# The self parts of a graph layer added to its residual in DRAM

## The reference, cut to what matters

```python
h = maximum(layernorm(x), 0)
x1 = x + (h @ W.T + bias)                 # W scattered from the edge weights
h = maximum(layernorm(x1), 0)
# two layers; A is the 1250 x 1250 matrix of edge counts, dinv = 1 / max(degree, 1)
h1  = relu(h  @ W_self0 + dinv * (A @ (h  @ W_neigh0)) + b0)
out =      h1 @ W_self1 + dinv * (A @ (h1 @ W_neigh1)) + b1
return x1 + out
```

## Time and profile before

| | |
|---|---|
| time, median of 3 runs | 789.57 us (789.22 to 791.21) |
| the profiled execution | 792.57 us, its span 790.7 us |
| TensorE matmul busy | 749.0 us, 95% of the span |
| VectorE busy | 576.4 us, 73% |
| GpSimd busy | 474.7 us, 60% |
| ScalarE busy | 354.8 us, 45% |
| mean granted TensorE clock | 0.987 of full |
| DMA | 148.82 MB, 188 GB/s over the span |

### The profile page before, as it was taken

How to read it: one execution, slowest core, us unless ns; L and a number is a source line. 1 busy time by engine, 2 the same in 40 slices (tenths; PEclk the granted TensorE clock), 3 DMA queues, 4 the chain that set the end, 5 groups by cost and what they waited for, 6 DMA issues and landing times.

```text
span 790.7 us, 13483 instructions
## 1 busy us (share of the span) xinstructions
PE 749.0 (95%) x4433; PEld 618.9 (78%) x4434; DVE 576.4 (73%) x813; ACT 354.8 (45%) x596; POOL 474.7 (60%) x593
## 2 busy tenths in 40 slices
PE   2878999999999999999998999999999999999998
PEld 2767888888878787788886888888878888877876
DVE  7989377778555799976676775446588867689595
ACT  7756743343244267632335655443222223245631
POOL 5000057666758899674765382417799765754884
PEclk9689999999999999999999999999999999999999
DMA  3112455865675862565865625966853668775277
GB/s 113 43 52 93 132 166 193 257 197 184 196 233 192 285 199 94 167 208 193 294 211 170 187 93 151 279 217 197 288 160 110 201 222 279 253 240 191 102 214 274
DMA packets 82877, 148.82 MB, mean 188 GB/s; under 512 B 10795, under 2 KB 20898, under 8 KB 82800
## 3 DMA queue, kind: packets, MB, share of 16 engines
q1 hardware_dynamic: 62862, 105.07, 42.4%
q10 hardware_dynamic: 19938, 42.79, 15.2%
HBM read 106.42 MB, written 41.41 MB: 187 GB/s over the span
## 4 chain that ended last, share of the span: by engine, by line
PE 69%; POOL 10%; DVE 10%; issue 7%; DMA 2%; ACT 1%; SPq 0%; POOLq 0%; DVEq 0%; ACTq 0%
PE bank L1713 33%; PE bank L1760 20%; PE bank L1647 12%; POOL split L1097 3%; DVE L L1943 3%; POOL T L1114 3%; DVE R L1928 2%; POOL T L1112 2%; DMA stage<-hT_scratch 2%; DVE L L1935 1%; POOL S L1083 1%; PE bank L1543 1%; PE bank L1559 1%; PE bank L1776 1%; PE bank L1640 1%
## 5 line engine op out<-in xcount | busy, mean ns | idle before, releaser
L1713 PE MATMUL bank<-slot,split 128*128 128x512 f32 x1680 | 386.7, 390 | 2.5 <-POOL split L1097 1.7
L1713 PEld LDWEIGHTS bank<-slot,split 128*128 128x128 f32 x1680 | 313.6, 188 | 69.4 <-issue 4.6
L1059 POOL TENSOR_TENSOR AT<-AT,az 128x50 int32 (+3 forms) x288 | 96.5, 335 | 121.6 <-DMA az<-asum_scratch 79.3
L1760 PE MATMUL bank<-slot,Ax 128*128 128x512 f32 x500 | 119.1, 392 | 2.4 <-DVE slot L2184 1.4
L1097 POOL TENSOR_TENSOR split<-stage,split 128x512 fp32r<-128x512 f32 x50 | 66.9, 1340 | 77.9 <-ACT split L1322 76.1
L1760 PEld LDWEIGHTS bank<-slot,Ax 128*128 128x128 f32 x500 | 92.9, 188 | 22.2 <-DVE slot L2184 1.8
L2080 DVE TENSOR_TENSOR slot<-T,slot 128x512 fp32r<-128x512 f32 x64 | 90.9, 1448 | 9.7 <-ACT slot L1313 8.3
L1647 PE MATMUL bank<-slot,split_m 128*128 128x512 f32 x320 | 91.1, 396 | 0.0
L1322 ACT CAST split<-stage 128x512 fp32r<-128x512 f32 x50 | 31.1, 623 | 121.9 <-PE bank L1713 74.2
L1114 POOL TENSOR_TENSOR T<-T,wst 128x512 f32<-128x512 f32 x48 | 68.7, 1447 | 4.6 <-DMA wst<-in_L_gnn_W_self 4.6
L1647 PEld LDWEIGHTS bank<-slot,split_m 128*128 128x128 f32 x320 | 58.5, 188 | 11.0
(11 more groups left out here) (219 smaller groups left out, 1124.7 us busy)
## 6 DMA issues: line engine op xcount, KB each, us to landing
stage<-hT_scratch SPq DMA_DIRECT2D x90, 256.0 KB, 3.5
wst<-in_L_gnn_W_neigh SPq DMA_DIRECT2D x56, 256.0 KB, 4.5
wst<-in_L_gnn_W_self SPq DMA_DIRECT2D x56, 256.0 KB, 3.3
x1b_scratch<-x ACTq DMA_DIRECT2D x10, 512.0 KB, 5.5
hT_scratch<-hTs ACTq DMA_DIRECT2D x10, 512.0 KB, 3.4
wst<-prod0g_scratch SPq DMA_DIRECT2D x20, 256.0 KB, 3.5
hT_scratch<-h1s ACTq DMA_DIRECT2D x20, 256.0 KB, 3.3
wst<-prod1g_scratch SPq DMA_DIRECT2D x20, 256.0 KB, 3.4
```

The source lines that it names most:

```text
L1059: pool.tensor_tensor(a, a, az32[:, n % NZ, pairs * pos:pairs * (pos + 1)], ALU.add) \
L1713: last = pe.matmul(dense_bank(v, which)[:, :], split[:, v % 2, a, NT * k:NT * (k + 1)], slot[t % 2][:, b, HF * (HK * which + k):HF * (HK * ...
L1760: last = pe.matmul(sums, Ax[:, u % NR_A, NT * k:NT * (k + 1)], part, start=(begins and k == 0 and b == 0), stop=(k == PAIRS - 1 and b == 1 ...
```

## The change

In the second layer the self parts are no longer stored to a scratch tensor of their own. GpSimd's queue issues a transfer for each that adds it to the x1 tile in DRAM (`dma_start` with `accum_op=ALU.add` into `x1b_scratch`), 20 of them with 256 KB each. `add_to_x1(v - 1)` stands at the end of GpSimd's iteration v, behind `right_lo`; the one for the last product stands behind the low parts of T2. It waits for VectorE to have taken product v - 1, and for the adding transfer two before it (`s_added` has two semaphores, used in turn). The A stage's `load_sums` loads one tile for each output, and `add_x1` and VectorE's L2264 are gone in it. Those who waited for a self store to free its source, namely VectorE in `sub_products`, `first_sums` and `take`, and ScalarE in `keep_first_A`, wait for the adding transfer. The stores of the neighbour parts and the first layer's stores stay on ScalarE's queue. In the first layer, a difference that counted a semaphore `s_a3` is counted as a link in VectorE's own chain, and ScalarE waits for the sum made from it in its place.

```diff
...
@@ -561,9 +560,20 @@
 
             return 16 * (PAIRS // 2 + 1 - i % 2) * (2 * layer + (p == 5)) + 16 * (i // 2 + 1)
 
-        def wait_c22(eng, layer, which, tiles):
+        def nth_added(half, n):
+
+            i = n % PAIRS
+            if half == n // PAIRS:
+                return PAIRS + 2 * i if half else i
+            return 3 * PAIRS + i if half else PAIRS + 2 * i + 1
+
+        def wait_added(eng, half, n):
+            m = nth_added(half, n)
+            eng.wait_ge(s_added[m % 2], 16 * (m // 2 + 1))
+
+        def wait_c22(eng, layer, tiles):
             for i in tiles:
-                eng.wait_ge(s_cst[2 * (i % 2) + which], cst_stored(layer, 5, i))
+                eng.wait_ge(s_cst[2 * (i % 2)], cst_stored(layer, 5, i))
 
         def dense_bank(v, which):
             return bank[2 * (v % VL % 3) + which]
...
@@ -867,22 +878,17 @@
                 elif o == 0:
                     sp.wait_ge(s_olo, VL * (layer + 1))
                     wait_low(sp, layer, "B11", PAIRS - 1)
-                if o == 0 and layer == 1:
-                    for r in range(2):
-                        sp.wait_ge(s_h1d[r], used(OL - 2 + r, 2))
-                    for i in range(TN - 2, TN):
-                        sp.wait_ge(s_x1d[i % 2], used(i, 2))
-                if half == 0 and n >= PAIRS:
-                    sp.wait_ge(s_c21, 16 * PAIRS * (layer + 1))
+                if layer == 1:
+                    wait_added(sp, half, n)
+                elif half == 0 and n >= PAIRS:
+                    sp.wait_ge(s_c21, 16 * PAIRS)
                 elif half == 1 and n < PAIRS:
-                    sp.wait_ge(s_c12[n % 2], c12_stored(layer, n))
+                    sp.wait_ge(s_c12[n % 2], c12_stored(n))
                 elif half == 1:
-                    wait_c22(sp, layer, 1, [n - PAIRS])
+                    sp.wait_ge(s_cst[2 * (n - PAIRS) % 4 + 1], cst_stored(0, 5, n - PAIRS))
                 else:
-                    sp.wait_ge(s_cst[2 * (n % 2) + 1], cst_stored(layer, 1, n))
-                sp.dma_start(sums_tile(layer, o), prod_d[layer][1][half, n]).then_inc(s_sl[o % NO], 16)
-                if layer == 1:
-                    sp.dma_start(x1_tile(o), x1b_d[n][:, HF * half:HF * (half + 1)]).then_inc(s_sl[o % NO], 16)
+                    sp.wait_ge(s_cst[2 * (n % 2) + 1], cst_stored(0, 1, n))
+                sp.dma_start(sums_tile(layer, o), self_part(layer, half, n)).then_inc(s_sl[o % NO], 16)
 
             def load_bias(layer):
 
@@ -1124,10 +1130,19 @@
                 high, low_part = right(layer, what, k)
                 pool.tensor_tensor(low_part, unsplit(what, k), high.bitcast(F32), ALU.subtract).then_inc(s_low_g, 1)
 
-            def add_x1(o):
-
-                pool.wait_ge(s_sl[o % NO], sums_loaded(1, o))
-                pool.tensor_tensor(sums_tile(1, o), sums_tile(1, o), x1_tile(o), ALU.add).then_inc(s_xadd, 1)
+            def add_to_x1(v):
+
+                layer, p, i = parts(v)
+                if layer == 0 or p not in (1, 5, 6):
+                    return
+                pool.wait_ge(s_evd, nth_sub(v) + 1)
+                from_cst, from_q = cst[:, 2 * (i % 2) + 1, :], q[:, p // 6, 1, i, :]
+                for half, n, source in {1: [(0, i, from_cst)], 5: [(1, i + PAIRS, from_cst), (0, i + PAIRS, from_q)],
+                                        6: [(1, i, from_q)]}[p]:
+                    m = nth_added(half, n)
+                    if m >= 2:
+                        pool.wait_ge(s_added[m % 2], 16 * (m // 2))
+                    pool.dma_start(self_part(1, half, n), source, accum_op=ALU.add).then_inc(s_added[m % 2], 16)
 
             def first_block_lo(b):
 
@@ -1155,8 +1170,11 @@
                         right_lo(layer, "B11", r - VL + 2 * PAIRS - 1)
                     if r >= VL - 2:
                         right_lo(layer, "T1", r - VL + 2)
+                    if v > VL * layer:
+                        add_to_x1(v - 1)
                 for k in range(PAIRS):
                     right_lo(layer, "T2", k)
+                add_to_x1(VL * (layer + 1) - 1)
                 for k in range(2, PAIRS):
                     right_lo(layer, "T1", k)
                 for k in range(PAIRS):
@@ -1164,13 +1182,8 @@
                 for k in range(PAIRS):
                     right_lo(layer, "T3", k)
                 for k in range(PAIRS):
-                    if layer == 1 and k < PAIRS - 1:
-                        add_x1(PAIRS + k)
                     right_lo(layer, "T4", k)
-                if layer == 1:
-                    for o in range(2 * PAIRS - 1, OL):
-                        add_x1(o)
-                else:
+                if layer == 0:
                     for b in range(WB):
                         first_block_lo(b)
                     operand_lo(VL)
...
@@ -1394,7 +1407,10 @@
 
                 p, i = A_SEQ[u]
                 act.wait_ge(s_ag, VL * layer + u + 1)
-                act.wait_ge(s_c12[i % 2], c12_stored(layer, i))
+                if layer == 1:
+                    wait_added(act, 1, i)
+                else:
+                    act.wait_ge(s_c12[i % 2], c12_stored(i))
                 act.copy(first_A(i), a_bank_of(u)[:, :]).then_inc(s_first, 1)
 
             def keep_first(v):
@@ -1409,17 +1425,17 @@
                 if p not in (1, 5, 6):
                     return
                 act.wait_ge(s_evd, nth_sub(v) + 1)
-                for which in range(2):
-                    dest = prod_d[layer][which]
-                    if p == 1 or p == 5:
-                        act.dma_start(dest[p // 5, i + PAIRS * (p // 5)], cst[:, 2 * (i % 2) + which, :]) \
-                            .then_inc(s_cst[2 * (i % 2) + which], 16)
-                if p == 5:
-                    act.dma_start(prod_d[layer][1][0, i + PAIRS], q[:, 0, 1, i, :]).then_inc(s_c21, 16)
-                if p == 6:
+                if p < 6:
+                    half, n = p // 5, i + PAIRS * (p // 5)
+                    act.dma_start(prod_d[layer][half, n], cst[:, 2 * (i % 2), :]).then_inc(s_cst[2 * (i % 2)], 16)
+                    if layer == 0:
+                        act.dma_start(prod_s_d[half, n], cst[:, 2 * (i % 2) + 1, :]).then_inc(s_cst[2 * (i % 2) + 1], 16)
+                if p == 5 and layer == 0:
+                    act.dma_start(prod_s_d[0, i + PAIRS], q[:, 0, 1, i, :]).then_inc(s_c21, 16)
+                if p == 6 and layer == 0:
                     if i >= 2:
-                        act.wait_ge(s_c12[i % 2], c12_stored(layer, i - 2))
-                    act.dma_start(prod_d[layer][1][1, i], q[:, 1, 1, i, :]).then_inc(s_c12[i % 2], 16)
+                        act.wait_ge(s_c12[i % 2], c12_stored(i - 2))
+                    act.dma_start(prod_s_d[1, i], q[:, 1, 1, i, :]).then_inc(s_c12[i % 2], 16)
 
             def h1_out(o):
                 u, half, n = OUTS[o]
...
@@ -2191,7 +2210,10 @@
                 dve.tensor_tensor(t1, t1, staged("a", k), ALU.subtract).then_inc(s_sum_g, 1)
                 wait_staged(dve, layer, "b", k)
                 if k == 0:
-                    dve.wait_ge(s_c21, 16 * PAIRS * (layer + 1))
+                    if layer == 1:
+                        wait_added(dve, 0, TN - 1)
+                    else:
+                        dve.wait_ge(s_c21, 16 * PAIRS)
                 dve.wait_ge(s_sum_g, sum_made(layer, "T1", k))
                 dve.tensor_tensor(t2, staged("b", k), t1, ALU.subtract).then_inc(s_sum_g, 1)
 
...
@@ -2260,10 +2281,6 @@
                 half, n = OUTS[o][1:]
                 sums = sums_tile(layer, o)
                 dve.wait_ge(s_sl[o % NO], sums_loaded(layer, o))
-                if layer == 1 and o < PAIRS:
-                    link(dve.tensor_tensor(sums, sums, x1_tile(o), ALU.add))
-                elif layer == 1:
-                    dve.wait_ge(s_xadd, o - PAIRS + 1)
                 if p == 1:
                     return
                 if p == 5:
...
```

More of the change, by code:

```diff
@@ L155, in build_program @@
     asum_d = nc.dram_tensor("asum_scratch", (NS_A, P, AW * TN), U16, kind="Internal").ap()
-    prod_d = [[nc.dram_tensor(f"prod{layer}{which}_scratch", (2, TN, NT, HF), F32, kind="Internal").ap()
-               for which in "gs"] for layer in range(2)]
+    prod_d = [nc.dram_tensor(f"prod{layer}_scratch", (2, TN, NT, HF), F32, kind="Internal").ap() for layer in range(2)]
+    prod_s_d = nc.dram_tensor("prod_self_scratch", (2, TN, NT, HF), F32, kind="Internal").ap()
     hT_d = [nc.dram_tensor(f"hT{layer}_scratch", (TN, P, KT, NT), F32, kind="Internal").ap() for layer in range(2)]
@@ L423, in build_program @@
         s_as = sem("s_as")
-        s_a3 = sem("s_a3")
         s_turn = sem("s_turn")
@@ L429, in build_program @@
         s_evb = sem("s_evb")
-        s_xadd = sem("s_xadd")
         s_degs = sem("s_degs")
@@ L487, in build_program @@
         s_c21 = sem("s_c21")
+        s_added = [sem(f"s_added{i}") for i in range(2)]
         s_c12 = [sem(f"s_c12_{i}") for i in range(2)]
@@ L843, in load_b11 @@
```

(21 more changed lines are left out.)

11 lines of the change are left out of this document (6 added, 5 removed).

## The result

The changed kernel takes 801.86 us (median of 6 runs, 799.62 to 803.3), the kernel before beside it 790.91 us (6 runs, 789.22 to 791.88). The ratio is 1.0137, 95% interval 1.0114 to 1.016: 10.9 us slower. The prediction was 799.3 us, slower, with a sum of +9.7 us; by these times the loss is 1.2 us larger than that sum. The profiled execution of the changed kernel took 799.83 us, its span 797.9.

What follows compares the result with a forecast made beforehand. TensorE was taken as the bound, GpSimd next to it. 2.7 + 7.5 + 0.5 - 1.0 = +9.7 us (13g - 3.3) on the profiled 792.57 gives 802.3, 799.3 us on the runs' median scale; own range 793 to 802, widened to 789 to 811.

Steps and rivals of the forecast that it cites:

- The hold g: Time for which one GpSimd transfer issue holds up what stands behind it; taken as 1.0 us, halfway between 0.45 and 1.6.
- Rival 1: The issue hardly holds GpSimd, working beside its tensor instructions: 788.6 us, or 790.6 at g = 0.33; chance 0.23.
- rival 3: VectorE stretches GpSimd's issues 1.35 times: g = 1.35, sum +14.3 us, 803.9 us; chance 0.14.
- Step 1: Second layer: three issues fall where GpSimd works nearly without a break before 2.4's low part; 3g - 0.3 = 2.7 us.
- Step 5: Ten issues, two in each iteration 5.1 to 6.0, make GpSimd the bound for five products; 10g - 2.5 = 7.5 us.
- the waits for landing: Each issue waits for the adding transfer two before; landing taken as 5.3 us, fits step 5; VectorE's `first_sums` delayed, +0.5 us.
- rival 2: Landing bounds step 5: an adding transfer takes 9.1 us, 3 us more for four iterations, +12, 811 us; chance 0.13.
- The start of the A stage: VectorE, some 2.7 us late from waiting in 6.0 for the last of ten transfers, delays it: +0.5 us, bounds 0 and 4.
- The gain (a): A stage without the adds of x1: the TensorE gap of 0.99 us at 761.79 goes, -1.0 us, bounds 0 and -1.0.

Runs made afterwards that it cites:

- e9_hold: Kernel before, no transfer on GpSimd's queue, three memsets (1.05 us together) at each of the twenty places of the adding transfers: 798.38 us, ratio 1.0111.
- e3_no1: Changed kernel without the five adding transfers of step 1 (their self parts missing from the result): 797.65 us, ratio 1.0094 to the kernel before.
- e4_no5: Changed kernel without the ten adding transfers of step 5 (their self parts missing from the result): 793.63 us, ratio 1.0042 to the kernel before.
- e11_b11: e1_four with the five low parts of B11 in the second layer's step 5 moved from GpSimd to VectorE: 794.85 us, ratio 1.0067.
- e1_four: Changed kernel with four semaphores for the adding transfers, so an issue waits for the one four before it: 798.27 us, ratio 1.0095 to the kernel before.
- e12_third: As e9_hold, with one memset (0.31 us) at each place in place of three: 791.59 us, ratio 1.0029.
- e5_nox1: Kernel before without x1 in the second layer's A stage, neither loads nor adds: 789.31 us against 790.22, ratio 1.0000.
- e2_plain: Changed kernel with GpSimd's transfers as plain stores into their own tensor, the A stage loading and adding x1 as before: 800.56 us, ratio 1.0118.
- e10_read: As e9_hold, with three copies that read SBUF at each place in place of the memsets: 805.46 us, ratio 1.0213.
- e8_gap_four: e1_four with the issues ahead of the low part in GpSimd's iteration, not at its end: 807.43 us, ratio 1.0225.

## Why the prediction was right, and where its terms were off

**The mechanism is shown.** GpSimd is held at its queue in two stretches where it has no time to spare, and its low parts come late. In step 5 the hold alone is enough for it, in step 1 the transfers bring something more. A hold without any transfer makes 8.2 us (e9_hold, some 6.9 of it at the issue's own length), taking the issues out of a stretch takes out that stretch's gaps (e3_no1, e4_no5), and giving GpSimd time back does it too (e11_b11).

**The hold g**, taken as 1.0, is 0.88, between the bounds of 0.45 (as on ScalarE's queue) and 1.6 (as a tensor instruction). It is the same for both sources, median 864 and 865 ns, and beside a busy VectorE or not: 0.86 us at 570.10, beside a subtraction of VectorE, and 0.86 at 690.11, with VectorE idle. Rival 1 needed less than 0.44 and is out, and so is rival 3, VectorE stretching the issues. The rule of the Trainium skill named there ("SBUF — State Buffer", "Who interferes with whom") agrees with these rows.

**Step 1, forecast 3g - 0.3 = 2.7, measured 3.08.** The place is right, though the loss is spread over the gaps in front of 2.2, 2.3 and 2.4 and not in one. With the measured g my sum gives 2.3, and the trace has even less in the stretch that I counted: from the low part of 1.4 to that of 2.4 it is 589.88 - 558.95 = 30.93 us, 28.85 before, 2.08 more for three issues. The other 1.0 us was there before this stretch began, where I had written that the earlier issues are absorbed. The low part of 1.4 ended 48.42 us after the layer's first matmul before, and ends at 49.41. ScalarE's high part in front of it, in the kernel before and in the changed one, and GpSimd's low part:

```profile
558.76 0.62 ACT L1322 CAST split<-stage 128x512 fp32r<-128x512 f32 x1 [5.79 <-DMA stage<-hT_scratch]
```
```profile
556.89 0.62 ACT L1335 CAST split<-stage 128x512 fp32r<-128x512 f32 x1 [6.78 <-DMA stage<-hT_scratch]
557.66 1.29 POOL L1103 TENSOR_TENSOR split<-stage,split 128x512 fp32r<-128x512 f32 x1 [2.09 <-ACT split L1335]
```

GpSimd's idle time of 1.86 us was a wait for ScalarE, and ScalarE's for an operand load. That load came 0.98 us later, and SyncE began the row of loads with it 0.73 us later (at +41.23 against +40.50). e4_no5, with the same issues in step 1, has it 1.2 us late. In e3_no1, without them, it comes as before (+0.03). In e9_hold, with the hold and no transfer, it comes 2.0 us earlier than before, and step 1 loses only 1.1 us. So it isn't the hold that delays the load. That leaves the transfers themselves, their traffic or their waits; these are single traces, and no run separates the two.

Something else is new behind the hold. VectorE's row and GpSimd's in the changed kernel:

```profile
571.93 4.66 DVE L2187 TENSOR_TENSOR q<-q,b 128x512 f32<-128x512 f32 x1
```
```profile
574.46 1.57 POOL L1103 TENSOR_TENSOR split<-S,split 128x512 fp32r<-128x512 f32 x1
576.50 1.84 POOL L1085 TENSOR_TENSOR S<-stage 128x512 f32<-128x512 f32 x1 [0.47 <-DMA stage<-hT_scratch]
```

The same add took 0.87 us in the kernel before. It now ends at 576.59, 0.56 us after GpSimd's row of instructions, without a break since 564.67, breaks off at 576.03. A late GpSimd runs without breaks, and then can hold up VectorE. In the stretch above, this add cost TensorE nothing that the three issues don't cover.

**Step 5, forecast 10g - 2.5 = 7.5, measured 6.93, and here two errors met.** The hold itself costs less than I had it. e1_four, which has the hold without landing waits, shows it: from 2.4 to the A stage 120.19 us against 114.73 before, less 1.37 us of lower clock after its gap at 590.55, is 4.1. Three terms were too dear. The smaller g makes 1.2 us for ten issues. GpSimd's four iterations from the sum of 5.2 on took 683.63 - 661.84 = 21.8 us before; in e1_four they are 6.80, 6.81, 6.31 and 6.34, together 19.2 without 1.76 for each pair of issues. That is 2.6 us shorter, where my sum had 1.3, since GpSimd found ScalarE's second high part ready in the last two, as at 681.67 in the changed kernel, where it follows its low part without a wait. The third term was put at nothing: the wait for ScalarE's first high part of this kind, ahead of the first pair of issues, which shrank from 2.71 to 1.60 us (659.56 above), because ScalarE has no self parts to issue in front of it; in e9_hold, where it has them, the wait is 2.65. In the kernel before:

```profile
660.60 1.29 POOL L1125 TENSOR_TENSOR g_mid<-base,g_mid 128x512 fp32r<-128x512 f32 x1 [2.71 <-ACT g_mid L1391]
...
683.63 1.30 POOL L1088 TENSOR_TENSOR stage<-stage,S 128x512 f32<-128x512 f32 x1
```

7.5 less 1.2, 1.3 and 1.1 is 3.9, beside the 4.1 of e1_four. And from 4.1, with ScalarE's issues back (1.1) and ten holds of 1.05 us for 0.88 (1.7), it is 6.9, beside the 7.39 of e9_hold. The times of e9_hold and e12_third point the same way: their 7.9 us for a microsecond of hold (6 to 12 by the two intervals) are less than the 13 of my sum.

What filled it up again is **the step "the waits for landing"**. I had taken 5.3 us to land and wrote that at 7.13 us an iteration "that fits". The median of 5.5 bears the first part out; but the transfers at 660.80 and 661.38, with a DMA share of 1.07 in the window from 667 (0.61 to 0.70 in the earlier trace rows), landed after 7.5 and 9.1 us, and GpSimd stood in front of the next two for 1.15 and 1.06 us. At 696.25 it stood once more, 1.89 us, and the gap in front of 6.3 follows from the low part behind it; e1_four has neither such a wait nor that gap. This is rival 2, in two iterations instead of four. It made the one gap of 2.96 us, and **the clock fell behind that gap**, 1.57 us that appear in no term of the forecast. So 6.93 is 4.1 for the hold, 1.6 for the clock and some 1.3 for the landing waits, the last as what is left. The gaps begin at 5.4 and reach 6.3, one product later than forecast.

**The start of the A stage, forecast +0.5, measured +1.19.** VectorE's wait for the last of the ten was 7.24 us, not the 2.7 + 1 or so that I had: that transfer was issued at 690.11 and landed after 6.9 us, not 5.3. VectorE caught up, but the last low part of B21 took it 4.75 us (713.77), beside four low parts of GpSimd end on end, and its two gaps are 0.82 + 1.27 us instead of the one of 1.42. The bounds 0 and 4 held.

**The gain (a), forecast -1.0, measured -1.23** over the rest of the A stage, with no gap at the place of the earlier trace rows: TensorE's matmuls go from 732.82 to 771.52 in one row. As a change by itself it is too small for the times to show (e5_nox1).

The sum came within 0.3 us of the trace's +9.97 since a hold that was too dear stood in for two costs that were missing: that closeness is luck, the direction and the places are not. Of what stays open: what about the transfers makes the operand load of 1.4 late, where the rest of e3_no1's 4.2 us comes from, and why behind similar gaps the clock falls in one run and not in another.

## What to carry to other kernels

Moving a queue's issues from one engine to another is a move of work: count each issue with its hold (here 0.88 us for an accumulating one of 256 KB, 0.55 for a plain one) against the time that the new engine has to spare in that very stretch, not against its share of busy time, which even fell. Give every wait on an earlier transfer the slowest landing that a full DMA stretch can give, not the median. And look at the granted clock behind a gap of TensorE before adding up gaps: here it fell behind single gaps from 2.23 us up.

## What the runs showed of the hardware that I had not expected

- An accumulating transfer from GpSimd's queue holds GpSimd for 0.86 us, a plain one of the same 256 KB for 0.55. They landed after 3.7, 5.5 and 9.1 us (least, median, longest), the plain ones after 2.3, 4.4 and 7.6.
- A VectorE add or subtraction of two SBUF tiles (0.7 us) took 4.66, 4.75 and, in e2_plain, 8.68 us while GpSimd ran SBUF-reading instructions end on end. It was blocked for the rest of that row, not for one instruction, and each time it ended 0.56 or 0.57 us after the row broke off. Beside another such row (578.30 to 582.96 in the changed kernel) the same add took 1.73 us; what decides between the two isn't shown.
- The clock fell to its lower level behind gaps of 2.23 us (e1_four), 2.29 and 2.40 (e10_read), 2.96 (changed kernel), 3.69 and 4.67 (e8_gap_four) and 6.52 (e2_plain). The loss was 1.4 to 1.6 us in the first five, 2.5 and 2.2 in the last two. It did not fall behind 2.75 (e3_no1) and 2.56 (e11_b11). It fell behind 0.85 and 1.27 us in close succession in e3_no1, and not behind 0.82 and 1.27 in the changed kernel. The gap's length alone doesn't decide it.
